# Two identity products for a causal mask, each moved from 128 rows of TensorE to a tile of 64 rows

## The reference, cut to what matters

```python
scores = jnp.einsum('bqhm,bkhm->bhqk', q, k) / jnp.sqrt(jnp.asarray(D_HEAD, q.dtype))
causal = jnp.arange(S)[:, None] >= jnp.arange(S)[None, :]
scores = jnp.where(causal[None, None, :, :], scores, jnp.asarray(IGNORE, scores.dtype))
pattern = jax.nn.softmax(scores, axis=-1)
```

## Time and profile before

| | us |
|---|---|
| median of 3 runs | 207.37 |
| lowest and highest | 206.98, 209.19 |
| the profiled execution, its own time | 209.23 |
| its span, first to last instruction | 207.7 |
| TensorE busy in the span | 191.9 |
| VectorE busy | 127.6 |
| ScalarE busy | 90.7 |
| GpSimd busy | 69.5 |

### The profile page before, as it was taken

One profiled execution on the slowest core, in us unless ns is written; L12 is line 12 of the kernel. 1 busy time (PEld: TensorE's weight loads), 2 busy tenths in 40 slices (PEclk: granted clock), 3 DMA queues, 4 the chain that ended last, 5 costly groups with the idle time before them and its releaser, 6 DMA issues.

```text
span 207.7 us, 4914 instructions
## 1 busy us (share of the span) xinstructions
PE 191.9 (92%) x1913; PEld 175.6 (85%) x1915; DVE 127.6 (61%) x391; ACT 90.7 (44%) x186; POOL 69.5 (33%) x111
## 2 busy tenths in 40 slices
PE   6897999999999999999999877999999999999960
PEld 1797898899799997889899763699999999999960
DVE  0058766666666035898797878348567458494183
ACT  2043560122544620372766913167747647643100
POOL 8423220013015100076576875610513523532000
PEclk9999999999999999999999999999999999999997
DMA  6989977005200000011000012384568758412713
GB/s 189 390 320 315 388 249 316 19 2 186 84 0 3 2 0 3 0 34 34 13 19 18 27 32 86 45 329 147 158 202 297 247 178 308 129 48 86 193 41 116
DMA packets 11814, 27.27 MB, mean 131 GB/s; under 512 B 3173, under 2 KB 7108, under 8 KB 10608
## 3 DMA queue, kind: packets, MB, share of 16 engines
q1 hardware_dynamic: 8976, 24.30, 34.8%
q0 software_dynamic: 2304, 2.21, 3.7%
q10 hardware_dynamic: 512, 0.46, 0.8%
HBM read 24.15 MB, written 5.77 MB: 144 GB/s over the span
## 4 chain that ended last, share of the span: by engine, by line
PE 81%; DVE 10%; DMA 2%; issue 2%; ACT 1%; POOL 1%; DVEq 0%; SPq 0%; ACTq 0%; POOLq 0%
PE ps L575 10%; PE ps L443 7%; PE ps L413 6%; PE ps L339 6%; PE ps L560 4%; PE ps L557 4%; PE ps L562 4%; PE ps L556 4%; PE ps L561 4%; PE ps L393 2%; DMA xp<-patches 2%; PE ps L395 2%; PE ps L396 2%; PE ps L397 2%; PE ps L394 2%
## 5 line engine op out<-in xcount | busy, mean ns | idle before, releaser
L861 POOL DMA_INDIRECT slots<-row,slot x16 | 18.9, 1181 | 30.8 <-issue 22.3
L892 POOL DMA_INDIRECT parts<-qT,toke x12 | 17.1, 1429 | 35.8 <-ACT qT L783 33.9
L1179 DVE TENSOR_TENSOR v<-v,ps 128x246 f32<-128x246 f32 x32 | 12.4, 408 | 16.3 <-ACT v L771 16.3
L575 PE MATMUL ps<-xp,v 128*123 128x192 f32 x128 | 22.0, 326 | 0.0
L1098 DVE TENSOR_TENSOR wqkv<-raw,wqkv 128x1024 fp32r<-128x1024 f32 x16 | 19.5, 1221 | 3.2 <-ACT wqkv L713 3.2
L575 PEld LDWEIGHTS ps<-xp,v 128*123 128x123 f32 x128 | 20.6, 186 | 0.0
L339 PE MATMUL ps<-convw,xp 128*98 128x192 f32 x96 | 18.9, 358 | 1.2 <-DMA xp<-patches 1.2
L339 PEld LDWEIGHTS ps<-convw,xp 128*98 128x98 f32 x96 | 17.0, 184 | 2.6 <-DMA xp<-patches 2.1
L674 ACT ACTIVATE prob<-sm 128x588 f32<-128x588 f32 x8 | 5.6, 705 | 29.7 <-DVE sm L951 29.7
L556 PE MATMUL ps<-zeA,wqkv 128*128 128x246 f32 x64 | 18.5, 290 | 0.0
L560 PE MATMUL ps<-zeA,wqkv 128*128 128x246 f32 x64 | 17.8, 279 | 0.0
(11 more groups left out here) (158 smaller groups left out, 484.9 us busy)
## 6 DMA issues: line engine op xcount, KB each, us to landing
raw<-w SPq DMA_DIRECT2D x8, 1025.0 KB, 6.5
xp<-w SPq DMA_DIRECT2D x8, 384.0 KB, 3.1
xp<-patches SPq DMA_DIRECT2D x8, 294.0 KB, 4.8
raw<-w_qkv SPq DMA_DIRECT2D x3, 768.0 KB, 4.9
slots<-blank SPq DMA_DIRECT2D x8, 196.0 KB, 4.9
xp<-slots SPq DMA_DIRECT2D x8, 196.0 KB, 4.4
parts<-zeros SPq DMA_DIRECT2D x1, 1176.0 KB, 9.4
part<-parts SPq DMA_DIRECT2D x4, 294.0 KB
```

The lines of the kernel that those rows point to most:

```text
L575: last = mm(ps[0:EROWS, 6 + r, 0:D], hT[:, j, jt, r * EROWS:(r + 1) * EROWS], w2s[:, j, jt, :], start=(jt == 0), stop=(jt == JT - 1))
L861: P.indirect_dma_start(slots, bass.IndirectOffsetOnAxis(slot[:, p % PH, k:k + 1], 0), row[:, p % 2, k, :], None, bounds_check=EXPERTS * ST ...
L892: P.indirect_dma_start(parts, bass.IndirectOffsetOnAxis(toke[:, e, r:r + 1], 0), ye[0:EROWS, e % 2, r, :], None, bounds_check=TOPK * N + E ...
```

## The change

The identity is replaced by four 64 x 64 identities, two side by side in rows 0 to 63 and two in rows 64 to 127. The product of rows 64b to 64b + 63 of this array with rows 64b to 64b + 63 of the mask gives 128 output partitions again, with the mask's 64 rows twice. Bank 0 gets this product over rows 0 to 63, and bank 1 over rows 64 to 127. Both are issued ahead of all 48 records of L413. For pairs 0 and 4 the first wait for keys is for four copies rather than three.

```diff
             def scores(p):
                 if p >= 1:
                     pe.wait_ge(sm_ready, p)
+                if p % PH == 0:
+                    pe.wait_ge(q_ready, HP * (p // PH + 1))
+                    pe.wait_ge(k_ready, HP * (p // PH) + 4)
+                for b in range(2):
+                    r = slice(SLOT * b, SLOT * (b + 1))
+                    mm(ps[:, b, 0:3 * PT], identb[r], causal[r], start=True, stop=False)
                 for hp in range(HP):
                     if p % PH == 0:
-                        if hp == 0:
-                            pe.wait_ge(q_ready, HP * (p // PH + 1))
-                        pe.wait_ge(k_ready, HP * (p // PH) + max(hp + 1, 3))
-                    if hp % 3 == 0:
-                        mm(ps[:, hp // 3, 0:3 * PT], identb, causal, start=True, stop=False)
+                        pe.wait_ge(k_ready, HP * (p // PH) + max(hp + 1, 4))
                     for i in range(2):
@@
-        "masking": np.concatenate([np.eye(128), np.tile(causal, (1, 2 * 3))], axis=1).astype(mybir.dt.np(mybir.dt.bfloat16)),
+        "masking": np.concatenate([np.tile(np.eye(SLOT), (2, 2)), np.tile(causal, (1, 2 * 3))], axis=1).astype(mybir.dt.np(mybir.dt.bfloat16)),
```

## The result

| | before | after |
|---|---|---|
| median of 4 runs, us | 208.28 | 213.23 |
| lowest, highest | 206.98, 209.27 | 211.89, 214.71 |
| the profiled execution: its own time, its span | 209.23, 207.7 | 214.71, 213.2 |
| its mean granted clock | 0.994 | 0.946 |
| ratio with 95% interval | | 1.0236 (1.0169 to 1.0303) |

The forecast was 205.3, with a range from 204.3 to 206.9. Yet the scores did what was forecast. TensorE's records of pair 3 of the changed kernel (start us, us, what; L422, L407 and L415 answer to L420, L408 and L413) stand here against those of pair 2 in the earlier trace rows; in both kernels pairs 2 and 3 cost the same within 0.01 us.

A forecast was written before the change was run, and what follows sets the result against it. TensorE was taken to bound the kernel; seven pairs saving 0.25 us and pair 5 saving 0.35 gave 2.10 us, taken from a median of 207.37 for 205.3 us, range 204.3 to 206.9.

The forecast's parts named there:

- What bounds the kernel, and the cost of a pair: Among the scores, distances between starts on TensorE count; a pair takes 1.96 us from first mask product to last score.
- The first rival: No drain between 64 x 128 and 64 x 64 tiles, or at the entry: another 0.8 us saved, 204.5; chance 0.15.
- The overlap (a): A pair's two 64-row mask products run at the same time, so the second adds 0.01 us; 0.12 if not.
- The second rival: The two mask products run one behind the other, costing 0.9 us in all: 206.2; chance 0.15.
- The merged scores: Without the mask product between a pair's two halves, the scores run as one group of 48 records, saving 0.36 us.
- The moved waits: Pairs 0 and 4 wait for the fourth copy of keys first; over a microsecond of cover at pair 4, cost nothing.
- Pair 5 and the sum: Pair 5 finds the array empty and saves 0.35 us; with 0.25 from each of seven others, 2.10 us on TensorE.
- The third rival: TensorE's waits for VectorE behind the attention take the saving back: 206.2 to 207.4, say 206.8; chance 0.10.
- "The experts behind are all TensorE. I take the whole.": Behind the attention nothing is lost, so the whole 2.10 us saved among the scores reaches the end.
- The slower rival: Half-row mask products are not pipelined with anything; first score 0.94 us away instead of 0.34: 210.3; chance 0.05.
- Theory A: Experiments' theory: the clock falls because of where the sparse stretch behind the attention comes; strong form, nearly all changed-kernel runs fall.
- C: Experiments' theory: whether the clock falls depends on timing that differs from run to run; the first four runs were unlucky.

The follow-up runs named there:

- e10: The kernel before with each mask product over 64 rows, still at its old place among the scores: 210.28 us, one time.
- e4: The changed kernel's order, but each mask product over all 128 rows: 208.48 us, ratio 0.9909 to the kernel before.
- e7: The kernel before without its 10 filler products behind the attention: 215.72 us, ratio 1.0335.
- e13: The kernel before with the two correction products of the values of pairs 0, 3 and 7 left out: 209.34 us, ratio 1.0021.
- e5: The changed kernel run again, nothing edited: 207.41 us, ratio 0.9926 to the kernel before.
- e14: The changed kernel run again, nothing edited: 207.47 us, ratio 0.9937 to the kernel before.
- e6: The kernel before run again with a new profile, nothing edited: 207.46 us.
- e3: The changed kernel with 10 filler products ahead of the transposes of pair 4, as a delay: 209.28 us, ratio 0.9999 to the kernel before.
- e9: The changed kernel run again, nothing edited: 208.22 us, ratio 0.9868 to the kernel before.
- e15: The changed kernel with 5 filler products ahead of the transposes of pair 4: 207.52 us, ratio 0.9952 to the kernel before.
- e1: The changed kernel with 13 fillers in TensorE's three waits and 9 instead of 6 behind the last: 207.44 us, ratio 0.9894 to the kernel before.
- e16: The changed kernel with only the 13 fillers inside the three waits: 205.02 us, ratio 0.9862 to the kernel before.
- e12: The kernel before with 16 added fillers, 13 in the three waits and 3 behind: 208.53 us, ratio 0.9969.

## Why the prediction was wrong

**What bounds the kernel, and the cost of a pair: right.** The price of a change of shape, 0.10 us each, held in every place: 128 x 128 to 64 x 128 (0.20 instead of 0.11 in after and e10), and 64 x 128 to 64 x 64 (0.23 from mask to score). The first rival, no price for one of them, is out. The Trainium skill, "TensorEngine Tiling (Array Packing)", "Key Properties", says that a change of the tiling mode drains the engine; these traces agree, for a change of rows alone too, with 0.09 to 0.10 us.

**The overlap (a): right.** Less than 0.01 us between the two mask products, 0.12 in e4 where they share rows. The second rival is out.

**The merged scores: right.** 48 records in 1.60 us, 1.38 from first to last as in the sum. Pair: forecast 1.71 from the mask's old start, measured 1.70 (0.09 + 0.23 + 1.38). The moved waits cost nothing.

**Pair 5 and the sum: right.** 2.10 forecast, 2.2 measured among the scores, 2.1 at the third wait. The third rival is out as well: the waits at L470 stayed 0.69, 0.69 and 1.07 us (before 0.69, 0.70 and 1.08).

**"The experts behind are all TensorE. I take the whole.": this step failed.** It took the length of the stretch behind the attention as fixed, and put the loss of clock there at nothing; it measured 8.0 us. I had read the clock as 1.00 "everywhere" from rows that leave out 104 to 135 us, and never asked what keeps it there. The clock was indeed 1.00 there in the trace of before, but TensorE's work was thin (same columns as the earlier trace rows):

```profile
121.00:127.00 6.00, 3.77 (x28) 2.25 (x26) 4.26 (x33) 1.75 (x5) 4.45 (x11) 1.00 0.22 56
```

The rest was at hand too: three waits of 2.5 us together at L468, and products on `filler` between them, which no result uses. e7 shows what they do: without them the clock fell in each of 6 runs. With them it is kept only just, since the kernel before loses it for long in 7 of 80 runs and for a short time in 54 of 76. The moment of the fall goes with its length. In the traces with the fillers as they were, a fall of 20 us began 1.49 us behind the end of the second wait (after), 1.50 (e13) and 1.55 (e5); the falls that began 1.79 (e10), 2.58 (e14) and 2.80 us (e6) behind it lasted 3.4 us; the traces of before, e3, e4, e9 and e15 had none there. That is an order among six traces, not a rule that was tested.

**The slower rival had the right sign and the wrong mechanism.** It looked for the loss in the half-row products (the way to the first score grew by 0.10 us, not by 0.6), and its chance was 0.05. A loss of the clock, which costs the kernel before 8 us in 7 of 80 runs, was no rival at all. Had the waits been read that way, the forecast would have held a second case near 213 us.

**What is not settled.** That a fall explains the slower runs is shown (trace and mean clock of each run, e1, e7, e16). That the change makes it *likelier* is not. 4 of 18 runs against 5 of 45 in the same jobs could be chance. The first job's 4 of 4 against 0 of 4 says more, and e9's 2 of 6 against 0 of 17 points the same way; e5 (1 of 6 against 3 of 17) and e14 (1 of 6 against 2 of 11) do not. e13 fell in 2 of 6 and e15 in 1 of 6, which fits either view. So the sign of the first comparison, four runs against four, may have been bad luck. Theory A stands in its weak form: the fall needs the sparse stretch. That timing decides whether it comes in a given execution (C) fits all runs but was not tested by itself.

## What to carry to other kernels

A saving on the bounding engine moves everything behind it; look for stretches there whose length isn't fixed by work, above all where TensorE is sparse and fillers hold its clock, and price their loss as a case of its own. If the clock hangs on them, put the filler products *inside* the waits (ahead of the waiting instruction), not only behind: here 13 of them cost nothing, were worth 0.7 to 0.9 us beside runs with only the short fall, and no run of the 44 that had such fillers fell. Where small tiles of one shape are broken up by a product of another shape, order alone can be worth more than packing: here each break cost 0.10 us going and 0.10 coming, and the packing itself brought only 0.02 per pair.

## What the runs showed of the hardware that was not expected

**Behind a sparse stretch the clock stayed down for 20 us of nearly full work.** In after TensorE had worked 1.64 of the 3 us before the clock fell, and it worked 19.82 of the next 20.4 us, yet the clock stayed down until 4 us into the dense products of the experts. In e14 the fall lasted 3.4 us; there most products of the gather came at full clock again. The busy share alone does not tell whether it falls: e15 had no fall with 2.52 of 4 us, before none with 2.12 of 4, and e6 fell after 3.75 of 5.7. None of the three waits of TensorE in after was over 1.1 us.

**Two groups of times, 2 us apart, in all kernels.** The chain of work that ended last begins with the 12 records of pair 0's embedding. In e5's trace, by start, us and what:

```profile
6.15 2.21 PE ps L339 x12
```

It was 4.17 us in before and 3.80 in after. The clock records kept with the traces begin with the rise to the upper level, at 4.5 us in e5 and at 10.7 and 9.3 in before and after; over all 18 traces it comes at 4.2 to 5.1 us (ten traces) or at 9.3 to 10.7 (eight). When it comes after the first load has landed at 6.1 us, the first 12 records last 3.8 to 4.2 us instead of 2.2, and all that follows is up to 2 us late. So a time of this kernel is one of two groups (208.0 to 208.5 or 209.8 to 210.1 in e12), plus the falls, and a median of four runs isn't enough to tell 1%.
